# Expert weights of a mixture-of-experts stage: which weight rows share a partition

## The reference

```python
top_probs, top_idx = top_k(softmax(x @ gate_w + gate_b), 2)     # 2 of 16 experts, renormalised
h1 = x @ w1[e]            # w1, w2: 16 x 256 x 512, float32
h2 = x @ w2[e]
hidden = silu(h1) * h2
expert_out = hidden @ w3[e]       # w3: 16 x 512 x 256, float32
```

## Time and profile before

| | |
|---|---|
| median of 3 runs | 3151.13 us |
| profiled execution | 3147.66 us |
| its span, first to last instruction | 3145.9 us |
| expert stage, first up to last down | 1057.7 to 1499.6 us |
| mean granted TensorE clock over the span | 0.783 |
| weight loads (L982) | 195 of 512 KB, median 4.8 us from issue to landing |

### The profile page before, as it was taken

How to read it: one execution, slowest core, us unless ns; L and a number is a source line. 1 busy time by engine, 2 the same in 40 slices (tenths; PEclk the granted TensorE clock), 3 DMA queues, 4 the chain that set the end, 5 groups by cost and what they waited for, 6 DMA issues and landing times.

```text
span 3145.9 us, 35365 instructions
## 1 busy us (share of the span) xinstructions
PE 2068.8 (66%) x10329; PEld 1614.2 (51%) x10329; DVE 1634.6 (52%) x5072; ACT 943.6 (30%) x2022; POOL 1537.8 (49%) x1544
## 2 busy tenths in 40 slices
PE   6599866776762588888335656565535656665599
PEld 5488644444442488888224444444424444444577
DVE  4110133333344244344637787777747787777554
ACT  4244200000000233333144444443433444442132
POOL 1100277777753200000657777774277777772243
PEclk9899866666665799899667787878858877778599
DMA  5244444444342478788344444443144444442000
GB/s 187 105 182 198 159 124 127 121 129 122 112 112 103 169 264 276 250 276 269 110 128 137 128 137 136 136 130 90 55 131 137 130 135 137 133 132 54 1 14 28
DMA packets 210379, 432.64 MB, mean 138 GB/s; under 512 B 34915, under 2 KB 117388, under 8 KB 203724
## 3 DMA queue, kind: packets, MB, share of 16 engines
q0 software_dynamic: 69280, 195.96, 22.6%
q1 hardware_dynamic: 131548, 225.86, 20.6%
q10 hardware_dynamic: 9360, 8.52, 0.8%
HBM read 343.69 MB, written 87.33 MB: 137 GB/s over the span
## 4 chain that ended last, share of the span: by engine, by line
POOL 31%; PE 30%; DVE 15%; issue 13%; DMA 9%; SPq 1%; DVEq 1%; ACT 1%; POOLq 0%; ACTq 0%
POOL arena L1231 15%; POOL arena L675 13%; PE banks L398 9%; DMA arena<-in_L_ffn_w_dram 6%; PE banks L1021 5%; PE banks L1335 3%; PE banks L1336 3%; DVE arena L1512 3%; DVE arena L1421 2%; PE banks L1033 2%; POOL xg L930 2%; DVE arena L1477 1%; PE banks L1719 1%; PE banks L1306 1%; PE banks L1803 1%
## 5 line engine op out<-in xcount | busy, mean ns | idle before, releaser
L1231 POOL DMA_INDIRECT arena<-ht,srcT x884 | 892.1, 1009 | 313.0 <-issue 266.0
L675 POOL DMA_INDIRECT arena<-tr,idx1T x442 | 422.3, 956 | 359.0 <-DMA tr<-arena 224.6
L1335 PE MATMUL banks<-arena,XT 128*128 128x264 f32 x884 | 374.6, 515 | 101.3 <-DVE arena L1512 59.7
L686 PE MATMUL banks<-arena 128*128 128x256 f32 x442 | 234.5, 628 | 178.2 <-DMA arena<-tr,idx1T 178.0
L1336 PE MATMUL banks<-arena,XT 128*128 128x264 f32 x884 | 345.3, 480 | 0.0
L1512 DVE TENSOR_TENSOR arena<-arena,nrmT 128x528 f32<-128x528 f32 x448 | 312.9, 704 | 21.0 <-ACT nrmT L1284 21.0
L398 PE MATMUL banks<-parts 128*128 128x512 f32 x1200 | 279.9, 396 | 49.9 <-DVE parts L426 49.9
L1021 PE MATMUL banks<-arena 128*128 128x128 f32 x2080 | 267.4, 290 | 67.9 <-DMA arena<-in_L_ffn_w_dram 67.6
L1335 PEld LDWEIGHTS banks<-arena,XT 128*128 128x128 f32 x884 | 216.2, 258 | 165.0 <-DVE arena L1512 65.4
L1021 PEld LDWEIGHTS banks<-arena 128*128 128x128 f32 x2080 | 256.5, 204 | 80.1 <-DMA arena<-in_L_ffn_w_dram 79.5
L711 DVE TENSOR_TENSOR X<-X,banks 128x256 f32 x221 | 92.3, 418 | 368.5 <-PE banks L687 367.8
(11 more groups left out here) (305 smaller groups left out, 3339.9 us busy)
## 6 DMA issues: line engine op xcount, KB each, us to landing
arena<-in_L_ffn_w_dram SPq DMA_DIRECT2D x195, 512.0 KB, 4.8
tr<-arena SPq DMA_DIRECT2D x50, 1024.0 KB, 3.9
XT<-dld SPq DMA_DIRECT2D x56, 512.0 KB, 4.5
arena<-ht,srcT POOLq DMA_INDIRECT x884
xg<-arena SPq DMA_DIRECT2D x13, 640.0 KB, 3.5
arena<-xg SPq DMA_DIRECT2D x65, 128.0 KB, 5.9
yg<-arena ACTq DMA_DIRECT2D x65, 128.0 KB, 4.8
arena<-tr,idx1T POOLq DMA_INDIRECT x442, 2.8
```

What stands on the lines that cost most here:

```text
L675: pool.indirect_dma_start(Gr[:, n, h, :], None, TR, bass.IndirectOffsetOnAxis(ap=idx1T[:, q:q + 1], axis=0)).then_inc(d_g[n], 16)
L686: ten.matmul(B[n][:, 0:D], OHr[:, n, 0, :], Gr[:, n, 0, :], start=True, stop=False)
L1231: pool.indirect_dma_start(G[c % NG4][:, j, :], None, HT[L], bass.IndirectOffsetOnAxis(ap=srcT[:, q:q + 1], axis=0)).then_inc(d_gat[c % NG4 ...
L1335: ten.matmul(B[n][:, 0:MSG], OH[b][:, 2 * j, :], G[c % NG4][:, 2 * j, 0:MSG], start=True, stop=False)
```

## The change

Two neighbouring rows of `w1` and `w2`, and four neighbouring rows of `w3`, now go to one partition: partition p holds rows 2p and 2p+1, or 4p to 4p+3. Each partition's part of a matrix is then one stretch of 4 KB in DRAM, as it is one in the buffer. For the products to stay the same, the turned rows must have the inputs in the same order, so the two transposes take every second column of `XGt`. The block h of hidden units must match the rows of `w3` held as number h, so the stationary operands of `pe_up` take every fourth column of `W1` and `W2`. `pe_down`, the casts and all waits are as they were.

```diff
-        wv = [a[n].rearrange("e (k p) h -> p e k h", p=P) for n in ("L0_ffn_w1", "L0_ffn_w2", "L0_ffn_w3")]
+        wv = [a[n].rearrange("e (p k) h -> p e k h", p=P) for n in ("L0_ffn_w1", "L0_ffn_w2", "L0_ffn_w3")]
@@ pe_turn_rows
-            ten.transpose(B[6 + c][:, 0:P], XGt[b][:, 0:P], ident[:, :])
-            ten.transpose(B[6 + c][:, P:2 * P], XGt[b][:, P:2 * P], ident[:, :]).then_inc(tn_ok, 1)
+            every = XGt[b].rearrange("p (q k) -> p k q", k=2)
+            ten.transpose(B[6 + c][:, 0:P], every[:, 0, :], ident[:, :])
+            ten.transpose(B[6 + c][:, P:2 * P], every[:, 1, :], ident[:, :]).then_inc(tn_ok, 1)
@@ pe_up
-                        mm = ten.matmul(B[bank][:, h * P:(h + 1) * P], W[b][:, k, h * P:(h + 1) * P], xTt[c][:, k, :],
+                        mm = ten.matmul(B[bank][:, h * P:(h + 1) * P], W[b].rearrange("p k (q h) -> p k h q", h=4)[:, k, h, :], xTt[c][:, k, :],
                                         start=(k == 0), stop=(k == 1))
```

## The result

The changed kernel takes 3303.74 us (median of 4 runs, 3302.91 to 3304.81), against 3151.27 us for the kernel before (median of 4) on the same chip: the ratio is 1.0487 with a 95% interval from 1.0469 to 1.0505. The forecast of 3136 us was wrong in sign; the rival "strided loads at half rate", with its 3304 us, is what came.

A forecast was written before the change was run, and what follows sets the result against it. The prediction took the expert stage to be a latency loop, half DMA and half TensorE. From 3147.66 us it took 15 for shorter loads, nothing for other terms: 3132.7 us profiled, 3136 us as median; range 3112 to 3308 us.

The forecast's parts named there:

- strided loads at half rate: Rival for pe_up's strided weight loads: 214 ns per load, 3.4 us more per up, +153 us, about 3300 us; chance 0.29.
- What bounds the kernel: Expert stage: a loop of latency, half DMA and half TensorE, with three buffers; pe_up waits 67.6 us for weights.
- The loads: Weight loads of the expert stage: 640 fewer packets per tile at 12 ns each, 15 us gained (11 to 38).
- the 31 rounds of the forecast: Expert stage: 62 loads inside the loop, two tiles per round, each round gaining 0.48 us, 15 us in all.
- Issuing: SyncE's issues of the weight loads: 373 ns falling to 319 ns, at most 3 x 0.05 us per tile, counted as nothing.
- The strided transposes: Two transposes per tile reading every second float: taken as no loss, with 7 us over 65 tiles as an end.
- The strided weights: pe_up's 32 weight loads per tile, reading floats 16 bytes apart: taken as no loss, following VectorE's strided row.
- The two ends: Bounds for one strided weight load in pe_up: nothing lost at 107 ns, or 214 to 266 ns if read twice.
- two sweeps: Mechanism supposed for pe_up's strided weight loads: each float is read twice, so a load takes 2 x 107 = 214 ns.

## Why the prediction was wrong

- *What bounds the kernel* held. It was a loop of latency with the DMA wait in it: taking down(j-3) out of it removed the wait.
- *The loads* had the right mechanism and a term too large. 640 packets per tile did go; the time fell by 10 us (6 to 14) where I had 15, and the waits from 66 to 58 us where I had about 50. What was mis-sized is the price of a packet: 12 ns taken, 6.4 to 7.1 ns by queue q1 itself, which with the 31 rounds of the forecast makes 8 to 9 us. My estimate of 4.7 ns from the Trainium skill, "DMA: Bandwidth & Descriptors", section "Why small descriptors are slow", was nearer than my 12, and its 6 us are at the edge of the interval. The 256 B of that section are said of putting descriptors together into one packet, not of longer runs, so they did not speak against this change.
- *Issuing*: 333 ns instead of 373 per issue, nothing on the path, as said.
- *The strided transposes*: their loads did take twice as long per column, and it did not reach the end.
- *The strided weights* are the step that failed, in the sentence "I take no loss, as the only strided row shows none". The term put at nothing measured 3.9 us per up (7.46 instead of 3.57 us), with a weight load of 330 instead of 192 ns. The position on the path had been read rightly: a load occupies 107 ns, a product follows every 114 to 120 ns, so there is no cover. The two ends had been set rightly too, 107 ns (nothing lost) and 214 or 266 ns for a load, and the measured distance from one product to the next, 7.46 / 32 = 233 ns, is between them. What failed was the choice by a row of another engine. VectorE reads one float every 132 bytes at about its contiguous rate; at the 1.9 ns per stretch that TensorE's weight loads need, 208 of them would have taken 395 ns, more than its whole 351. That row says nothing about TensorE's weight loads.
- *The rival* gave 9.2 us per tile and +153 us; measured are 9.17 us and +152 us by the medians. That it is so close is luck. It put 3.4 us for the stride where 3.9 came, and added it to 5.75 us, a tile at the mean clock of 0.96, where a tile at clock 1.00 takes 5.27 (the kernel with earlier loads); the changed kernel ran at 1.00, and the two errors cancel. At clock 1 throughout the rival itself had 8.9 us and +137. Its mechanism was not quite the one told either. Not two sweeps through the same floats, but a fixed time per 16 bytes touched fits all five strides; with two sweeps a product's load at stride 2 would have taken twice a transpose's, and it took 113 ns where those took 113 and 124.
- The chances were 0.50 to 0.36 on the wrong side, and the range, drawn up to 3308 us to take in the rival, holds the 3304 us. The forecast itself was faster by 15 us, and the kernel became slower by 152.

## What to carry to other kernels

A layout that gives a DMA longer runs can put a stride on an operand of TensorE. Count the 16-byte stretches that each weight load then touches, at about 1.9 ns each as in this kernel, and compare with the distance between products: here 640 packets per tile saved 10 us and 32 strided loads per tile cost 160. Where a stage waits for loads, look first at which event frees the buffer; here an earlier one was worth 81 us, the better layout 10, and the layout nothing once the loads were early.

When a cost has no row of its own, the row of another engine is not a nearest row; the bound that the operation's own engine gives (a load already at its limit) should weigh more.

## What the runs showed of the hardware that I had not expected

- A weight load on TensorE takes about 1.75 to 1.95 ns per 16 bytes touched, beside 84 ns, with strides of 8, 12, 16 and 32 bytes in products and of 4 and 8 in transposes; a float32 product's load has in addition a least time of 107 ns, which a transpose's has not (56 ns).
- A load with a stride of 16 bytes hardly depends on the granted clock. In the changed kernel the first up, at a mean clock of 0.76, took 7.71 us and the next, at 1.00, 7.46; in the kernel before such a pair is 5.59 us at 0.66 and 3.57 at 1.00. By these means each first up had some 3.8 us at the lower level, my estimate, which cost the one 0.25 us and the other 2.
- Issuing one of these DMAs takes SyncE a median of 333 ns in the changed kernel, against 373 ns before.
- The kernel before took 3679.54 us in one series of runs and 3140 to 3151 us in the others, once on a chip of the same number; the excess of some 537 us lies outside the stage studied here. The cause is open.
